# Two transfers at other points of a part, and twelve warm-up products of 64 columns for four of 256

## The reference

```
xn = layernorm(x)
q, k, v = xn @ Wq.T, xn @ Wk.T, xn @ Wv.T          # 16 heads of 16
y = (q k^T * gamma**(i-j) / 4, for i >= j) @ v      # 4 x 1024 positions
yn = (y - mean) / sqrt(var + eps)                   # per batch and head
x1 = x + (yn * gn_weight + gn_bias) @ Wo.T
z = layernorm(x1)
shared = (silu(z @ sw1 + sb1) * (z @ sw3 + sb3)) @ sw2 + sb2
out = x1 + (shared + (expert_a(z) + expert_b(z)) / 2) / 2   # gelu experts, picked by token number
```

## Time and profile before

| | |
|---|---|
| median of 3 runs | 431.55 us (431.1 to 432.46) |
| the profiled execution's own time | 431.59 us |
| its span, first to last instruction | 429.8 us |
| PE busy | 419.1 us, 98% of the span |
| DVE busy | 335.3 us, 78% |
| ACT busy | 219.2 us, 51% |
| POOL busy | 87.9 us, 20% |
| moved by DMA | 39.79 MB |
| granted TensorE clock, mean | 1.000 |

### The profile page before, as it was taken

One profiled execution on the slowest core, in us unless ns is written; L12 is line 12 of the kernel. 1 busy time (PEld: TensorE's weight loads), 2 busy tenths in 40 slices (PEclk: granted clock), 3 DMA queues, 4 the chain that ended last, 5 costly groups with the idle time before them and its releaser, 6 DMA issues.

```text
span 429.8 us, 14531 instructions
## 1 busy us (share of the span) xinstructions
PE 419.1 (98%) x6232; PEld 380.5 (89%) x6232; DVE 335.3 (78%) x791; ACT 219.2 (51%) x420; POOL 87.9 (20%) x78
## 2 busy tenths in 40 slices
PE   7998999999999989999999999999999999999997
PEld 5987899999998989998989988899888998888996
DVE  7888689876987788987798887978879878856423
ACT  3566667555754568345257325483344834346530
POOL 3062634532344232650510000100001000000000
PEclk9999999999999999999999999999999999999999
DMA  8554444434351232315450015100142001120011
GB/s 262 192 150 139 126 151 116 114 104 133 123 169 51 87 115 89 101 53 195 158 187 2 2 49 190 56 0 1 49 152 91 0 1 49 49 98 0 2 50 49
DMA packets 19769, 39.79 MB, mean 93 GB/s; under 512 B 3040, under 2 KB 5376, under 8 KB 19200
## 3 DMA queue, kind: packets, MB, share of 16 engines
q1 hardware_dynamic: 19280, 38.31, 27.5%
q10 hardware_dynamic: 432, 0.66, 0.5%
HBM read 30.55 MB, written 8.41 MB: 91 GB/s over the span
## 4 chain that ended last, share of the span: by engine, by line
PE 96%; issue 1%; DVE 1%; DMA 1%; POOL 0%; ACT 0%; DVEq 0%
PE bank L434 54%; PE bank L443 13%; PE bank L526 7%; PE bank L444 7%; PE bank L556 4%; PE bank L571 4%; PE bank L540 3%; PE bank L505 2%; PE bank L589 1%; DMA xin<-xa 1%; PE bank L647 0%; PE bank L461 0%; PE bank L452 0%; DVE xlo L1311 0%; DVE ln_st L1298 0%
## 5 line engine op out<-in xcount | busy, mean ns | idle before, releaser
L434 PE MATMUL bank<-x2lo,sw_hi 128*128 128x512 f32 x128 | 50.5, 394 | 0.0
L434 PE MATMUL bank<-x2hi,sw_lo 128*128 128x512 f32 x128 | 50.2, 392 | 0.0
L434 PE MATMUL bank<-x2hi,sw_hi 128*128 128x512 f32 x128 | 50.1, 392 | 0.0
L443 PE MATMUL bank<-w_both,ehi 128*128 128x512 f32 x124 | 45.1, 397 | 0.0
L887 ACT ACTIVATE sil<-bank,s1b 128x512 f32<-128x512 f32 x32 | 22.0, 687 | 45.0 <-PE bank L434 44.9
L443 PE MATMUL bank<-sw_both,ghi 128*128 128x512 f32 x124 | 44.9, 396 | 0.0
L1199 DVE STREAM_TRANSPOSE x2t<-xl 32x256 f32<-32x256 f32 x96 | 41.8, 436 | 1.8
L768 ACT ACTIVATE kexp<-bank 64x256 f32<-64x256 f32 x64 | 24.2, 378 | 30.9 <-PE bank L505 30.2
L1029 DVE TENSOR_TENSOR pm<-bank,msk 128x512 f32<-128x512 f32 x64 | 39.5, 679 | 0.0
L434 PE MATMUL bank<-xhi,wqkv_hi 128*128 128x256 f32 x128 | 38.0, 297 | 0.1
L906 ACT ACTIVATE ehi<-xres 128x512 fp32r<-128x512 f32 x32 | 20.3, 633 | 33.1 <-PE bank L444 32.6
(11 more groups left out here) (154 smaller groups left out, 1152.0 us busy)
## 6 DMA issues: line engine op xcount, KB each, us to landing
w_raw<-w SPq DMA_DIRECT2D x16, 256.0 KB, 3.3
xres<-xs SPq DMA_DIRECT2D x16, 256.0 KB, 3.4
x_scratch<-xres SPq DMA_DIRECT2D x16, 256.0 KB, 3.3
xl<-x_scratch SPq DMA_DIRECT2D x8, 512.0 KB, 4.5
xr<-x_scratch SPq DMA_DIRECT2D x4, 1024.0 KB, 4.8
xin<-xa SPq DMA_DIRECT2D x15, 256.0 KB, 3.0
out<-xr SPq DMA_DIRECT2D x7, 512.0 KB, 2.6
xin_t<-xt SPq DMA_DIRECT2D x13, 256.0 KB, 2.6
```

Source lines behind the costliest of these rows:

```text
L434: mm = nc.tensor.matmul(o, w[c][l], x[c][r], start=first and c == 0 and j == 0, stop=last and c == n - 1 and j == 2)
L443: nc.tensor.matmul(o.rearrange("p (k d) -> p k d", k=2), hi, w[c], start=c == 0, stop=c == n - 1, skip_group_check=True)
```

## The change

Three edits. On SP, load_rstd waits for k_done of the next part as well. Still on SP, in parts 8, 9, 12 and 13 the first of the two xres transfers is issued behind a wait for s_done and no longer at the part's end. On PE, the four warm-up products of 256 columns become twelve of 64 columns.

```
-WARM_UP = 4
+WARM_UP = 12
...
                 if TURNED <= h + 2 < PARTS:
+                    sp.wait_ge(k_done, h + 2)
                     load_rstd(h + 2)
...
                 if h in LOAD_STEPS:
                     load_ffn(2 + LOAD_STEPS.index(h), 1)
+                if b >= 2 and s < 2:
+                    sp.wait_ge(s_done, h + 1)
+                    next_xres(b - 1, 2 * s)
                 if h + 1 < PARTS:
                     sp.wait_ge(kt_done, h + 2)
...
                 if b >= 2 and s < 2:
-                    next_xres(b - 1, 2 * s)
                     next_xres(b - 1, 2 * s + 1)
...
             def warm_up(n):
                 for _ in range(n):
-                    nc.tensor.matmul(c_bank[:, 0:2 * P], zeros[:, 0:P], zeros[:, 0:2 * P], start=True, stop=True)
+                    nc.tensor.matmul(c_bank[:, 0:CH], zeros[:, 0:P], zeros[:, 0:CH], start=True, stop=True)
```

## The result

The change took 432.02 us (median of 22 runs, 430.68 to 433.85), and the kernel before, run in turn with it on the same chip, 430.70 us (22 runs, 429.79 to 434.56). The ratio is 1.003 with a 95% interval of 1.0015 to 1.0044. The change is slower, by about 1.3 us. I had forecast 430.9 us and no change that can be told. The time lies in my range and the sign is wrong.

A forecast was written before the change was run, and what follows sets the result against it. PE's work plus its stops at 256-instruction pages bound the kernel. −0.75 (pages) + 0 + 0 + 0.1 (warm-up) = −0.65 us gave 430.9 us from the median 431.55, no measurable change; range 428.6 to 433.1.

The forecast's parts named there:

- pages: PE's blocks of 256 instructions: 32 more instructions move their boundaries, stops go from 4.84 to 4.1 us, term −0.75 us.
- rstd_row: SP's load of rstd_row waits for the key projection; DVE still gets it in time: cost 0.
- xres: Four transfers of 256 KB go out after the state sums, 4 to 7 us sooner: worth 0.
- The step that failed: the warm-up itself: Twelve thin products at the start end before DVE is ready at 6.16 us, clock rising as before: 0.1 us tail.
- 0.174 us a record: Warm-up at the start: beyond this pace the idle time until 6.16 us no longer covers it and it costs.
- rival C: Start: thin warm-up frees the clock later, transposes to first key projection slow; +1.5 us on −0.75, 432.3 us; chance 0.13.
- others: Remaining pages with 3 to 4 us of work and a transfer ahead of them: new stops of 0.8 us together.
- the first one in the list: Page at 36.60: 4.26 us of work instead of 2.87, entered before 640 KB reach the engines; 2.32 us stop goes.
- the formula: PE's stop at a page is the packet's delay + 2.4 us − PE's own time for the page.
- rival A: Pages come out well: two large stops go, new ones total 2.0 us; 2.8 us less, 428.7 us; chance 0.25.
- Rival B: Bulk transfers ahead of packets at 95.55 and 119 us; stops 6.5 to 7 us, +2 us, 433.5 us; chance 0.12.
- Rival D: Crossings are hidden, stops have another cause and stay at 4.84 us on both sides: 431.65 us; chance 0.05.

The follow-up runs named there:

- twin without a queue: The change with 4 warm-up products of 64 columns and 8 of 32 by 64, instead of twelve of 64 columns: 431.27 us, 1.0027 to the kernel before.
- The kernel with 128 columns: The change with twelve warm-up products of 128 columns instead of 64: 430.96 us, 0.9997 to the kernel before.
- the 32 increments: The kernel before with 32 increments of an unused semaphore on PE ahead of the warm-up: 437.44 us, 1.0154.
- experiment 3: The kernel before with 8 small products of 32 by 64 zeros behind its old warm-up, 32 more PE instructions: 433.37 us, 1.0055.
- change again: The changed kernel as it is, measured a second time against the kernel before: 432.46 us, 1.0056.
- experiment 5: The kernel before with 4 warm-up products of 64 columns instead of 256: 432.01 us, 1.0034.

## Why the prediction was wrong

The sum was −0.75 (pages) + 0 (rstd_row) + 0 (xres) + 0.1 (warm-up). The runs give, from one kernel to the next: transfers −1.5 us (0.9964), pages on top of them +1.2 (0.9991), thin warm-up on top of that +1.7 (to the change's 1.003) or +2.8 (to its 1.0056 the second time). Together +1.3, or +2.4. These are steps between kernels of different groups. The first can be told from nothing, the second cannot (+1.2, give or take 1.5), the third can (give or take 1.2 for the one and 1.3 for the other). That the time came to lie in my range is luck: a gain of the transfers and a loss by the pages, neither of them so in my sum, nearly cancel, and what is left is a term that I had at 0.1.

**The step that failed: the warm-up itself.** "I take 0.1 us for a tail", and "If the rise came as before the term is 0". It was 1.7 to 2.8. Both parts of it were off. *The queue*: I bounded a record by its columns (0.11 us) and by an uncovered load of 0.16, taken from one record of 797 ns beside a median of 634. That difference was no price of a load. Records overlap, so what one costs is the step from its start to the next one's, and that was 213 ns. The warm-up ended at 7.4 us by the chain, beyond my upper bound of 5.9. The price is 1.0 us at the first scores and 1.2 in the medians (the change against its twin without a queue). I had written down the point from which it decides, 0.174 us a record, and the bound that should have told me was too low. *The clock*: it is worth about 1.0 us alone (four thin products, 1.0034) and about 1.5 on top of the new pages (1.0027 for 0.9991). The kernel with 128 columns splits the two otherwise. It has the queue without the late clock and lies 0.3 us above the one with neither (0.9997 for 0.9991), and the change lies 1.4 to 2.5 us above it. So the sum of queue and clock is measured, and their shares only to about 1 us. This is rival C, with a chance of 0.13 and a price of 1.5 us. It was right in mechanism, place and size: "if the key projection shows 213 ns a product (C)", and 13 products at 221 ns stood there. That its 432.3 us lies so near the measured 432.02 is partly luck, since it holds −0.75 for the pages and nothing for the queue. The Trainium skill (TensorE: Matmul & The Clock Gate, Part 1) says that only sustained activity frees the clock; the runs agree in direction. All warm-ups but one began at 2.0 us; with those of 64 columns the clock rose at 9.5 to 12.0 us in five executions, with the one of 128 at 8.0, and with that of 256 between 5.1 and 8.1 in ten. With the 32 increments ahead, that of 256 began at 5.7 us and the clock rose at 11.8. I had the rule beside the forecast and gave it a chance of 0.13 and no part in the sum.

**The pages' sign.** The places were right: the stops lie where the count put them. Their sizes, in us (the kernel with the new pages and old transfers is that of experiment 3; a stop under 0.15 is a dash):

| stop in the prediction | predicted | new pages, old transfers | change | change again |
|---|---|---|---|---|
| 24 (page at 19.72) | 0.9 | 0.23 | 0.19 | - |
| 37 (in "others") | | - | 0.42 | 1.62 |
| 41 (page at 36.60) | 0 | 1.48 | 1.20 | - |
| 73 (page at 70.59) | 0.4 | 0.27 | 0.27 | 0.82 |
| 98 (page at 95.55) | 1.5 | 2.30 | 0.58 | 0.24 |
| 131 (page at 127.96) | 0.5 | 0.54 | 0.27 | - |
| 158 (page at 153.62) | 0 | 0.47 | - | - |
| others | 0.8 | 0.28 | - | - |

The stop at 159.94 us of experiment 3 stands in the row of 158: it cuts the products of line 571 after 46 of 64, where the one of 1.40 us did after 62, 32 instructions later. The two columns on the right are one program in two executions. Their stops differ from place to place, and in part 2 (37 and 41) they sum to 1.62 both times, as in the column before them: where one packet has been waited for, the next comes in time. The failed assumption is the first one in the list: "it is entered before the 640 KB have reached the engines. The stop of 2.32 us goes." It became 1.48 in the kernel before with new pages and 1.20 in the change. In the changed kernel PE entered that page at 39.44 us, and SP's timeline of it has:

```profile
39.45 0.36 SPq L301 DMA_DIRECT2D xres<-xs  x1
39.85 0.43 SPq L289 DMA_DIRECT2D w_raw<-w  x1
41.17 0.33 SPq L282 DMA_DIRECT2D rstd_row<-rstd_scratch  x1
```

and its packet is seen at 42.78 us (the DMA view of its window 42.7:42.8):

```profile
q8 instruction: 1, 0.02, 60.7%
```

3.35 us after the page was entered, and behind transfers that were issued at that time or later. 3.35 + 2.4 − 4.56 is 1.19, and 1.20 was measured: the formula holds, the delay I put into it does not. My starting point was off too: I took the 4.84 us of one execution for the kernel's own, and a kernel with the same pages and transfers had 3.05 (experiment 5). Either the packet is asked for later than at the page's first instruction, or engines that serve both take the bulk first; no run tells these two apart. The changed kernel's stops came to 2.93 us and not 4.1, near rival A. The moved transfers have most likely shortened them: with the new pages the sums are 3.46, 4.55 and 5.71 us in three executions with the old transfers, and 2.68 to 3.51 in five with the new ones. Rival A's mechanism was there, its gain was spent at the start. Rival B's price, +2 us, is what the pages cost with the old transfers (+2.5), by stops of 5.7 us and not 6.5 to 7, and by dips that I did not know of. Rival D is out: the stops moved with the instructions. Of the Trainium skill's word (Runtime: NRT & Kernel Launch, Instruction fetch mechanics) that crossings are mostly hidden I had said that it does not hold here. By their number it does: queue q8 moved 44 packets in the change, and 2 to 8 stops of 0.1 us or more stood in an execution. The few that show cost 1.4 to 5.7 us together in the 17 executions that I read.

**The transfers' nought.** I priced the waits (right: DVE waits for rstd_row once in each execution of the change, 0.3 and 0.6 us, and 0.4 in the kernel before) and not what I had just said of packets: that a transfer issued later leaves the way free. I counted xres on those grounds and rstd_row not. The runs show rstd_row's part as 0.7 to 2.2 us by the two ratios, and xres' as 0.4, which its interval doesn't tell from nothing. That it works through the stops is argued from sums in two executions of either kind (4.99 and 3.05 us without the wait, 2.71 and 2.36 with it), and not shown packet by packet.

**What stays open.** Why a dip comes in one execution and not in the next, and why the change, which has the new pages too, has so few; and the parts do not add to better than 1 us: the warm-up alone measured +6 us (six runs, of which five had a dip), more than with the moved transfers.

## What to carry to other kernels

Warm the clock with wide products (those of 256 columns did best here), and let them end before the first real product can start: price a record at its measured step from start to start, not at its columns. Where an engine runs through its instructions quickly, count where its 256-instruction boundaries fall and what bulk transfer is in the way just then; holding back one transfer by a wait that costs nothing was worth 0.7 to 2.2 us here, and no other warm-up that I tried was faster than the old one. Read several executions of each kernel before a stop of 1 or 2 us is called its own.

## What I had not expected of the hardware

- **The clock falls again in the middle of the work.** Three profiled executions show a granted clock of 0.50, which is 1.2 GHz, for 3.41 us each: in the warm-up-alone kernel at 41.26, in that of 128 columns at 38.75 and in that with rstd_row behind q_done at 117.15 us. They began 1.3 us behind the end of a stop of 1.90, 1.1 us into one of 1.52, and 2.4 us behind the end of one of 0.75 us. Runs with a lower mean clock were about 2 us longer (432.8 against 430.4 in the kernel before). That the stop causes it is argued from three cases; against it stand stops of 1.65 us, of 2.32 in the kernel before and of 2.30 in the kernel with new pages, without a dip in their executions.
- **Narrow products with 128 columns of float32 weights keep a pace of 213 ns at 1.2 GHz**, for 64 and for 128 columns alike; that the weight load sets it at 64 is argued. With 32 columns of weights 16 records took 0.66 us, 41 ns each.
- **The same program's clock rises at other times.** With the warm-up of 4 products of 256 columns that begins at 2.0 us it rose between 5.13 and 8.1 us in ten executions. The first scores began between 13.19 and 13.63 us in them. In two executions of the change it rose at 12.02 and 10.74 us, and their key projections took 5.83 and 5.27 us.
- **A semaphore increment on PE is not free**: 32 of them put the warm-up from 1.98 to 5.68 us. That makes an estimate of 0.12 us each by the delay (3.70/32), and of 0.18 if they began with the span (5.68/32).
